# One list of tasks, x 5.7 steps sooner, and pack transfers that carry two heads

## The reference

```python
for lvl in range(LEVELS):
    x = query[:, ::2 ** lvl, :]
    outs.append(_mha(x, in_proj_w[lvl], in_proj_b[lvl], out_w[lvl], out_b[lvl]))
current = outs[-1]
for lvl in range(LEVELS - 2, -1, -1):
    current = _upsample_linear(current, outs[lvl].shape[1])
    current = current @ up_w[lvl].T + up_b[lvl] + outs[lvl]
```

```python
h = silu(tlin(x, w1, s1)) * tlin(x, w2, s2)
h = gelu(tlin(h, h1, t1)); h = gelu(tlin(h, h2, t2)); return tlin(h, w3, s3)
```

## Time and profile before

| | |
|---|---|
| median of 3 executions | 3859.89 us (3854.78 to 3865.58) |
| profiled execution | 3860.58 us, span 3857.9 us |
| TensorE busy | 3553.0 us, 92% of the span |
| ACT busy | 2603.8 us, 67% |
| DVE busy | 2570.0 us, 67% |
| POOL busy | 1135.9 us, 29% |
| mean granted TensorE clock | 0.961 |

### The profile page before, as it was taken

The page is one execution under the profiler, slowest core; times in us unless marked ns, Lnnn a source line. Parts: engine busy times, 40 slices in busy tenths (PEclk is TensorE's granted clock), DMA queues, the critical chain, the costliest instruction groups (busy, mean ns, idle before and its releaser), DMA issues. The chain is left out here.

```text
span 3857.9 us, 59432 instructions
## 1 busy us (share of the span) xinstructions
PE 3553.0 (92%) x20995; PEld 1437.0 (37%) x20995; DVE 2570.0 (67%) x4836; ACT 2603.8 (67%) x3274; POOL 1135.9 (29%) x1068
## 2 busy tenths in 40 slices
PE   5899989989989989988998998949999999999998
PEld 3333333333333323333332332224445444444444
DVE  6778888888887897897897888933333343333333
ACT  2778878878878877877987887844444444444443
POOL 2244443454353353454454344220000000000000
PEclk6899989989989998998998999979999999999999
DMA  4423323332332332232342332210000000000000
GB/s 144 156 75 96 117 78 96 101 102 78 99 110 80 101 108 87 88 115 75 95 116 84 93 104 92 72 58 1 23 12 12 12 21 14 12 12 13 21 12 12
DMA packets 229951, 269.87 MB, mean 70 GB/s; under 512 B 53316, under 2 KB 189572, under 8 KB 229024
## 3 DMA queue, kind: packets, MB, share of 16 engines
q1 hardware_dynamic: 220400, 257.10, 22.5%
q10 hardware_dynamic: 9216, 8.39, 0.6%
HBM read 159.75 MB, written 101.45 MB: 68 GB/s over the span
## 5 line engine op out<-in xcount | busy, mean ns | idle before, releaser
L976 ACT ACTIVATE a_probs<-a_p_s,a_unit_now 128x1024 f32<-128x1024 f32 x1360 | 1445.4, 1109 | 301.3 <-PE a_p_s L1301 296.6
L1081 DVE TENSOR_REDUCE a_part_max<-a_p_r 128x1 f32<-128x512 f32 x2048 | 1303.4, 677 | 240.0 <-PE a_p_r L1314 237.1
L1314 PE MATMUL a_p_r<-a_k_st,a_q_st 48*128 48x512 f16 (+2 forms) x2944 | 912.6, 380 | 159.7 <-DVE a_part_max L1081 99.8
L1673 PE MATMUL p_h<-f_h_hi,f_w_hi 128*128 128x512 f16 x2048 | 776.3, 379 | 3.0 <-issue 1.6
L1673 PE MATMUL p_h<-f_h_lo,f_w_hi 128*128 128x512 f16 x2048 | 776.2, 379 | 0.0
L1331 PE MATMUL a_p_o<-a_probs,a_v_aug 128*17 128x512 f32 (+2 forms) x5888 | 739.3, 582 | 2.8 <-ACT a_raw L986 2.2
L1301 PE MATMUL a_p_s<-a_q_st,a_k_st 50*128 50x512 f16 (+2 forms) x2944 | 699.8, 374 | 45.4 <-ACT a_probs L976 40.6
L1314 PEld LDWEIGHTS a_p_r<-a_k_st,a_q_st 48*128 48x128 f16 x2944 | 224.0, 94 | 1185.7 <-DVE a_part_max L1081 847.9
L1535 ACT ACTIVATE f_h_f<-p_h,f_sc_now 128x512 f32<-128x512 f32 x256 | 175.9, 687 | 517.0 <-PE p_h L1673 515.0
L1081 DVE TENSOR_REDUCE a_row_max<-a_p_r 128x1 f32<-128x512 f32 (+2 forms) x672 | 429.0, 677 | 98.0 <-PE a_p_r L1314 94.8
L1482 POOL TENSOR_TENSOR f_rstd<-f_var_eps,f_minus_half 128x1 f32<-128x1 f32 x64 | 35.9, 561 | 1240.4 <-DVE f_var_eps L1628 1240.4
(11 more groups left out here) (157 smaller groups left out, 4741.5 us busy)
## 6 DMA issues: line engine op xcount, KB each, us to landing
qk_scratch<-a_qk_room SPq DMA_DIRECT2D x288, 128.0 KB
a_w_lo<-wqkv_inner SPq DMA_DIRECT2D x30, 768.0 KB, 4.5
a_q_st<-qk_scratch SPq DMA_DIRECT2D x64, 192.0 KB, 3.6
...
```

Of the source, the lines that this page charges most:

```text
L976: act.activation(probs[:, s % 2, 2 * p:2 * p + 2, :], p_s[:, 2 * p:2 * p + 2, :], ACT.Exp, scale=unit_now[:, lvl:lvl + 1]).then_inc(exp_do ...
L1081: dve.reduce_max(out, src, AX.X).then_inc(max_read.sem, 1)
L1314: ins = pe.matmul(p_a[:, r * size:(r + 1) * size], q_st[rows_of(j, ROWS), query_at:query_at + 128], k_st[rows_of(j, ROWS), key_at:key_at + ...
L1673: ins = pe.matmul(out, a, c, start=first and n == 0, stop=last and n == len(terms) - 1)
```

## The change

CUT_POINT and the windows go: all tasks of all batches are one list with absolute times, sorted once for each engine, and the banks are dealt in one pass. X_AT = 21.3 puts x of the next batch at -63.71, 5.65 steps sooner, and what is placed relative to it moves too: the x cuts, weights and span tasks by 5.65 steps, the first projections by 5, those of level 1 by 7 to 6, of level 0 by 6 to 8. The registers' form of an iteration (a pair) is gone with `number` and `earlier`. x of a batch waits for the copy of that batch alone.

The feature rows of levels 2 and 3 are dealt in another order (the rows of `out_w` are reordered on entry to match), so that two heads that lie side by side in `attn` have the same 16 partitions and the two halves of the 256 features. One pack transfer then carries both: 4 transfers instead of 8 for a unit of level 2, 8 instead of 16 for unit 6. The two cuts of level 2 become one over both halves.

```diff
-CUTS = [Cut(2, 0, 0, 256, (0,)), Cut(2, 1, 0, 256, (1,)), Cut(1, 0, 0, 512, (2, 3)), ...
+CUTS = [Cut(2, None, 0, 256, (0, 1)), Cut(1, 0, 0, 512, (2, 3)), ...
-PACKS = [HG * across(unit.lvl) for unit in UNITS]
+PACKS = [2 * HG if unit.lvl == 3 else HG for unit in UNITS]
+def feature_row(lvl, head):
+    if lvl < 2:
+        return head // 8, head % 8
+    j, i = divmod(head % (HG * across(lvl)), across(lvl))
+    if lvl == 2:
+        return i, HG * (head // 8) + j
+    return i % 2, 2 * j + i // 2
-CUT_POINT = 26.9
+X_AT, FIRST_END = 21.3, 20.9
-    load_at = {...} if first else {2: CUT_POINT - STEPS + .05}
+    load_at = {...} if first else {2: X_AT - STEPS}
-    before = [...]; body = window(CUT_POINT, CUT_POINT + STEPS, range(2)); end = [...]
+    tasks = [(at, kind, 0, n) for at, kind, n in opening if (kind, n) in early or kind == "xcopy"]
+    tasks += [(it * STEPS + (last_at(kind, n, at) if it == N - 1 and at >= FIRST_END else at), kind, it, n)
+              for it in range(N) for at, kind, n in regular if it or at >= FIRST_END]
-                                sp.wait_ge(x_copied.sem, 16 * (B - 1))
+                                sp.wait_ge(x_copied[it - 1].sem, 16)
+                            at = A_AT[unit.lvl] + unit.blk * W
                             for j in range(HG):
-                                for i in range(parts):
-                                    head = unit.head + j * parts + i
-                                    at, to = A_AT[unit.lvl] + unit.blk * W, (head % 8) * 16
-                                    sp.dma_start(a_lo[to:to + 16, head // 8, at:at + size].bitcast(F32),
-                                                 attn[32 * j:32 * j + 16, n % RING, i * size:(i + 1) * size]).then_inc(packed[n % RING].sem, 16)
+                                for i in range(0, parts, 2):
+                                    c, group = feature_row(unit.lvl, unit.head + j * parts + i)
+                                    chunks = min(parts, 2)
+                                    sp.dma_start(a_lo[group * HD:group * HD + HD, c:c + chunks, at:at + size].bitcast(F32),
+                                                 attn[32 * j:32 * j + HD, n % RING, i * size:(i + chunks) * size].rearrange("p (c t) -> p c t", c=chunks))\
+                                      .then_inc(packed[n % RING].sem, 16)
```

180 lines of the change are left out of this document (76 added, 104 removed).

## The result

The changed kernel takes 3834.11 us (median of 4 runs, 3830.77 to 3839.98), the kernel before 3862.51 us (4 runs, 3854.78 to 3865.58): ratio 0.9934, 95% interval 0.9915 to 0.9953. It is faster by 28 us, where 57 were forecast. The profiled execution took 3839.98 us, 1.8 of them around its span, at a mean granted clock of 0.962; that of before had 0.961.

A forecast was written before the change was run, and what follows sets the result against it. No engine bound the disturbed steps 24 to 34; late x starved TensorE and halved its clock, while TensorE bound step 35 onward. 7 x 7.0 + 5.5 + 2.5 = 57 us gave 3804 us, forecast range 3785 to 3818.

The forecast's parts named there:

- sum for steps 24 to 34: Eleven steps of each batch from 0 to 6: 37.5 + 1.5 + 3.8 = 42.8 instead of 49.8, 7.0 us a batch.
- TensorE loses the half clock: Steps 24 to 34: TensorE at full clock needs 32.6 us instead of 41.3, with the V pair 33.9.
- 16 packs hold SP, x comes late, ACT and DVE stop in order at their x tasks, TensorE starves, its clock halves: Around step 24 of seven batches: cause given for TensorE's 4.67 us idle and 17 to some 20 us at clock 0.50.
- 42.8 us a batch: Forecast length of steps 24 to 34: ACT's 37.5 us plus waits of 1.5 and 3.8, against 49.8 before.
- rival B: Clock falls again in steps 24 to 27: 3 to 10 us low, costing 1.5 to 5 a batch; about 3828; chance 0.20.
- C: Rival: waiting for the second reach product halves the clock for 20 us over steps 26 to 31; 3888; chance 0.06.
- ACT as the floor: Steps 24 to 34: ACT bounds the stretch with 37.5 us, 36.0 plus 1.5 for one `a_w_hi` from step 41.
- The wait for `a_reach`: Second reach product, behind `a_w_lo` on POOL, delays step 26's exponentials by 3.8 us, bounds 0 and 6.2.
- Packs: Levels 2 and 3: 16 transfers each become 8 in a batch, 0.63 us an issue kept, 5.0 us of SP saved.
- Batch 7: Last batch: SP free 5.0 us sooner moves neg and W3 weights by 4.1, plus half the slow clock: 5.5 us.
- Batch 0: ACT's 6.38 us wait for a store of q and k, behind 8 packs; four of them go: 2.5 us.
- Later projections and V: Moved 7 to 8 steps forward inside steps 35 to 84: 0, bounds a loss of 1.5 and a gain of 1.3.

The follow-up runs named there:

- e1: Changed kernel with X_AT back at 26.95: packs as changed, x and its work at the old place; 3839.9 us, ratio 0.9943.
- e4: Changed kernel with GpSimd's first `a_w_lo` in three instructions of 512 columns; 3827.0 us, ratio 0.9909.
- e7: Changed kernel with both `a_x_top` 0.6 step later on VectorE and GpSimd's first `a_w_lo` in three instructions; 3826.7 us, ratio 0.9905.
- e14: Changed kernel with the four spans one step later; 3834.5 us, ratio 0.9926. Its pair: batches 2 and 3, same code, 43.3 and 47.9 us for steps 24 to 34.
- e17: e14 with every score matmul of steps 24 to 27 of batches 0 to 6 done twice; 3820.6 us, ratio 0.9892.
- e18: e14 with VectorE's two `a_x_top` 0.6 step later; 3828.2 us, ratio 0.9908.
- e12: e4 with each `a_x_top` reading 16 of its 512 columns from batch 1 on, leaving out part of the computation; 3827.4 us, ratio 0.9911.
- e6: Changed kernel with VectorE taking both `a_x_top` 0.6 step later; 3834.1 us, ratio 0.9923.
- e3: Changed kernel with the packs, cuts and feature rows of before; only x and its work at the new place; 3840.3 us, ratio 0.9951.
- e8: Changed kernel with every score matmul of steps 22 to 28 of batches 0 to 6 done twice; 3835.5 us, ratio 0.9926.
- e9: e7 with every score matmul of steps 22 to 28 of batches 0 to 6 done twice; 3836.7 us, ratio 0.9934.
- e16: Changed kernel, x and first weights loaded at 21.29, x's work at its old place, spans one step later, second `a_x_lo` six steps later; 3823.4 us, ratio 0.9890.
- e13: e4 with GpSimd's second `a_x_lo` six steps later; 3824.7 us, ratio 0.9900.

## Why the prediction was right in its chain up to the last link, and wrong in its sum

**The step that failed** is in the sum for steps 24 to 34: "TensorE loses the half clock". The chain behind it, "16 packs hold SP, x comes late, ACT and DVE stop in order at their x tasks, TensorE starves, its clock halves", holds up to its last link, "its clock halves". The long idle went from 4.67 to 2.33 us as the chain said, and the half clock stayed. e1 takes the late transfer away and keeps 17.1 us of it. Nor is any long idle needed: in batches 5 and 6 of the changed kernel, 4 to 6 of e4, 3 and 4 of e7 and 4 of e14 the clock falls with no TensorE idle above 0.67 us in the 10 us before. The forecast 42.8 us a batch is near what the steps take where the clock comes back soon, with 3.4 to 7.7 us at half clock in them: 42.8 to 44.4 in five batches of e17, 43.1 to 43.8 in four of e14, 41.9 to 42.6 in three of e18. The batches of the same three kernels that have 13.7 us or more of it in one piece take 45.6 to 47.9. The changed kernel has that in all of batches 1 to 6 and takes 46.3, which is 3.5 more than forecast; by e14's pair 13.7 us at half clock cost 4.6. That 42.8 fits the short cases so well is in part luck: its 3.8 us for `a_reach` did not come in the changed kernel, its 37.5 us of ACT are 36.2, and the short cases still have some half clock in them. Every batch with x's work in it has some, in all the traces.

**The rival B** ("the clock falls again for a while", about 3828) was the case that came, with a length that only C had: 13.7 to 20.5 us. C put 20 us of it at 12 us a batch; at the pair's third of a us for each they are 7, so that the loss which C worked out never came. B came near the time, 3828 against 3834, by two errors that cancel: the half clock was longer than its 3 to 10 us and cheaper than its half of a us for each.

**ACT as the floor** was never reached: ACT is busy 35.6 to 36.4 us in batches 1 to 6 of all variants, against 37.5 in the forecast, and the steps take 41.9 us at the best. The second `a_w_hi` came in as said, but one of the two `a_x_hi` now stands before the first exponential of step 24. The forecast noticed that and counted its time all the same.

**The wait for `a_reach`**, 3.8 us with bounds of 0 and 6.2, was not seen in the changed kernel. Its place had `a_x_top` twice (TensorE idle 2.33 us) and `a_unit_qk`, held for 2.81 us. That the wait for GpSimd stands right behind them e12 shows, with 2.62 us. e4 prices `a_unit_qk` at 1 us a batch. Which of these stops it is matters little: e6, e7 and e12 exchanged one for another and won nothing. No edit took all of them away.

**Packs.** The wait of x fell as said, and e1 and e3 show that the packs alone or the early load alone do it. SP's 8 transfers of unit 6 took 5.12 us where 16 took 9.99, 0.64 each: the kept 0.63 was right, though each now carries two heads. Batch 7 was sized at 5.5 us: its steps 24 to 34 went from 40.5 to 33.9, 6.6 us, all at full clock now:

```profile
2332.39:2366.34 33.95, 28.90 (x196) 7.18 (x193) 31.14 (x57) 30.91 (x37) 13.24 (x12) 1.00 0.28 71
```

With the packs alone, in e1, they take 36.5, a gain of 4.0. In the changed kernel the batch lost 2.5 in steps 0 to 23 and some in its later ones, so that it gained 2.7 in all. Batch 0's steps 0 to 19 gained 2.9 where 2.5 were forecast (ACT's wait for the store of q and k, 6.38 us in the earlier trace rows, is now shorter):

```profile
138.39 0.63 ACT L944 ACTIVATE a_qk_room<-a_qk_room 128x512 f16<-128x512 f32 x1 [4.00 <-DMA qk_scratch<-a_qk_room]
```

**Later projections and V** were put at 0. Without half clock in them steps 35 to 84 take 169.3 us against 169.9, inside the bounds of 1.5 and 1.3: the later steps lost 2.1 and the last eight won 2.7. What was not in the sum are the short falls at step 35, which cost up to 2.7 us in three batches.

In the profiled execution, which is 20.6 us faster than that of before, 36 us are missing of the 57. 23 of them are steps 24 to 34 of batches 1 to 6 (6 x 3.8, the 7.0 less the 3.2 won), 7 the other steps of these batches, with the short falls at steps 4, 23 and 35, 3.4 batch 0 (6.1 won of 9.5), 2.8 batch 7, and what is left, under 1, lies ahead of and behind attention.

What stays open is why the clock falls in these steps at all, and why it comes back after 3.4 us in one batch and after 17.1 in the next with the same code and the same idle before it. e17 speaks for more TensorE work in these steps making the short kind more frequent; e8 and e9, with other orders, show that it doesn't always. Whether the kernel would spread as e14 does with other inputs wasn't tried.

The best versions, e17 (3820.6), e16 (3823.4) and e13 (3824.7), beat both kernels. Their intervals to each other overlap.
